# First row's broadcast load turned into columns of the small table, epsilon as a third group of the moments, padded token added by VectorE's multiplication

## The reference

```python
x = einsum(patches, conv_w) + conv_b            # 256 tokens of 128 per image, 2048 products each
for i in range(2):                              # two layers
    y = _ln(x); q, k, v = y @ qkv_w[i]          # layer norm, eps = 1e-5 under the root
    q = softmax(q, -1) * scale; k = softmax(k, -2)
    x = x + (q @ (k.T @ v)) @ out_w[i] + out_b[i]
    x = x + gelu(_ln(x) @ ff1_w[i] + ff1_b[i]) @ ff2_w[i] + ff2_b[i]
h = _ln(x) @ head_w + head_b                    # 192 wide
# linear attention of 12 heads, with one padded token whose phi(k) is 1 everywhere
z = 1 / (phi(q) . (sum of phi(k) over 256 tokens and the padded one) + EPS)
h = h + (q, kv, z) @ W_out + b_out              # of _layernorm(h)
h = h + proj(gelu(fc(_layernorm(h))))           # weights scaled by mixed alpha_e * alpha_r
```

## Time and profile before

| | us |
|---|---|
| median of three runs | 139.9 (138.65 to 140.72) |
| profiled execution, its own time | 139.65 |
| its span, first to last instruction | 137.9 |
| busy: TensorE products | 120.1 (87%), 938 instructions |
| busy: weight loads | 106.2 (77%) |
| busy: VectorE | 79.6 (58%), 231 instructions |
| busy: ScalarE | 66.6 (48%) |
| busy: GpSimd | 54.3 (39%), 65 instructions |
| mean granted TensorE clock | 0.975 of full |

### The profile page before, as it was taken

One profiled execution on the slowest core, in us unless ns is written; L12 is line 12 of the kernel. 1 busy time (PEld: TensorE's weight loads), 2 busy tenths in 40 slices (PEclk: granted clock), 3 DMA queues, 4 the chain that ended last, 5 costly groups with the idle time before them and its releaser, 6 DMA issues.

```text
span 137.9 us, 2475 instructions
## 1 busy us (share of the span) xinstructions
PE 120.1 (87%) x938; PEld 106.2 (77%) x938; DVE 79.6 (58%) x231; ACT 66.6 (48%) x149; POOL 54.3 (39%) x65
## 2 busy tenths in 40 slices
PE   6995699997899898998989989479984989999992
PEld 6985698796687686877777877269962878999991
DVE  0000406999579747795559944673858698356001
ACT  4000312951769966599667996028222140751420
POOL 0000270053649726587246764576293340022000
PEclk9999869999999999999999999977999999999999
DMA  4978999802950000000000000000000000000101
GB/s 127 392 297 324 409 415 410 309 11 84 324 127 0 0 2 5 0 0 5 0 0 0 0 7 0 0 0 2 5 0 0 0 0 0 0 5 0 57 0 57
DMA packets 4091, 11.63 MB, mean 84 GB/s; under 512 B 464, under 2 KB 1712, under 8 KB 4080
## 3 DMA queue, kind: packets, MB, share of 16 engines
q1 hardware_dynamic: 4080, 11.48, 23.0%
HBM read 11.09 MB, written 0.39 MB: 83 GB/s over the span
## 4 chain that ended last, share of the span: by engine, by line
PE 44%; DVE 31%; DMA 8%; issue 6%; POOL 5%; SPq 3%; ACT 2%; DVEq 0%; POOLq 0%
PE bank L329 14%; DMA patches_sb<-in_patches 8%; PE bank L596 5%; PE bank L487 4%; PE bank L463 4%; DVE nkmax L752 4%; DVE q L764 4%; DVE nqmax L759 4%; PE bank L353 3%; POOL qn L1157 3%; DVE xn L686 3%; PE bank L455 2%; DVE qsum L771 2%; SPq L278 2%; DVE ktok L780 2%
## 5 line engine op out<-in xcount | busy, mean ns | idle before, releaser
L1134 POOL TENSOR_TENSOR rstd<-var,minus_half 128x2 f32<-128x2 f32 x14 | 9.9, 705 | 44.8 <-DVE var L681 44.8
L1157 POOL TENSOR_TENSOR qn<-q,rqsum 128x512 f32<-128x512 f32 x8 | 8.2, 1042 | 10.5 <-DVE rqsum L776 10.5
L1011 ACT ACTIVATE kexp<-bank,nkmax 128x256 f32<-128x256 f32 x16 | 7.4, 471 | 7.2 <-DVE nkmax L752 6.9
L353 PE MATMUL bank<-embed_sb,patches_sb 128*128 128x128 f32 x64 | 9.6, 315 | 1.2 <-DMA patches_sb<-in_patches 1.2
L353 PEld LDWEIGHTS bank<-embed_sb,patches_sb 128*128 128x128 f32 x64 | 9.1, 227 | 1.4 <-DMA patches_sb<-in_patches 1.4
L353 PE MATMUL bank<-embed_sb 128*128 128x128 f32 x64 | 8.6, 294 | 1.5 <-DMA embed_sb<-in_embed 1.4
L463 PE MATMUL bank<-cw,qT 128*128 128x128 f32 x64 | 10.0, 288 | 0.0
L353 PEld LDWEIGHTS bank<-embed_sb 128*128 128x128 f32 x64 | 8.3, 207 | 2.0 <-DMA embed_sb<-in_embed 1.9
L463 PEld LDWEIGHTS bank<-cw,qT 128*128 128x128 f32 x64 | 8.2, 190 | 1.6 <-issue 0.8
L1006 ACT ACTIVATE qkvw_hi<-qkvw 128x512 fp32r<-128x512 f32 x3 | 1.9, 630 | 14.9 <-DMA qkvw<-in_qkv_w 14.9
L732 DVE TENSOR_TENSOR x<-bank,first_sb 128x128 f32<-128x128 f32 x4 | 1.0, 284 | 13.5 <-PE bank L353 13.5
(11 more groups left out here) (138 smaller groups left out, 333.5 us busy)
## 6 DMA issues: line engine op xcount, KB each, us to landing
patches_sb<-in_patches SPq DMA_DIRECT2D x4, 512.0 KB, 11.8
embed_sb<-in_embed SPq DMA_DIRECT2D x2, 768.0 KB, 6.3
restw<-in_rest_w SPq DMA_DIRECT2D x2, 768.0 KB, 14.1
embed_sb<-in_embed SPq DMA_DIRECT2D x2, 384.0 KB, 8.7
qkvw<-in_qkv_w SPq DMA_DIRECT2D x3, 256.0 KB, 10.6
embed_sb<-in_qkv_w SPq DMA_DIRECT2D x1, 768.0 KB, 4.5
embed_sb<-in_embed SPq DMA_DIRECT2D x1, 576.0 KB, 3.9
projw_raw<-in_proj_w SPq DMA_DIRECT2D x1, 576.0 KB, 14.8
```

What stands on the lines that cost most here:

```text
L353: mm = nc.tensor.matmul(EMB[i][t][:, 0:D], patches[:, t * P:(t + 1) * P], embed_sb[:, c, 0:D], start=(c == 0), stop=(c == KCONV - 1))
L1011: nc.scalar.activation(kexp[i][:, c, :], KB[c // 2][:, (c % 2) * TOKENS:(c % 2 + 1) * TOKENS], ACT.Exp, bias=nkmax[i][:, c:c + 1], accum_o ...
L1134: nc.gpsimd.tensor_tensor(rstd[i][:], var[i][:], minus_half[:], ALU.pow).then_inc(rstd_ready[i], 1)
L1157: nc.gpsimd.tensor_tensor(qn[i][:, t, :].rearrange("p (h d) -> p h d", h=HEADS), q[i][:, t, :].rearrange("p (h d) -> p h d", h=HEADS), rqs ...
```

## The change

Three edits. The row of 134 floats becomes 134 more columns of the small table, repeated on the host for each partition; the table grows from 248 to 382 columns, its load moves from after the sixth embed piece to after the fourth, and the broadcast load is gone. `bn_stats` writes into the first six of nine numbers a tile; the last three are a third group (count 0, mean 0, sum of squares width x epsilon), set once at the start in one buffer for each of the two widths, so that `bn_aggr` gives variance plus epsilon; the addition and its semaphore are gone, and GpSimd waits for `bn_aggr` itself. The one-row product is gone; VectorE computes (sum + 1) x q in one instruction.

```diff
-        small_sb = sb("small_sb", [P, P + EC + NCOL])
+        small_sb = sb("small_sb", [P, NSMALL])                  # NSMALL = P + EC + NCOL + NALPHA + D
-        first_sb = sb("first_sb", [P, NALPHA + D])
+        conv_b = small_sb[:, CONV_B_AT:NSMALL]
-        stats = per_image("stats", [P, TILES, 6])
+        stats = {D: per_image("stats", [P, TILES, 9]), E: per_image("stats3_", [P, TILES, 9])}
-        var = per_image("var", [P, TILES])
...
-                if j == CONV_PIECES - 2:
-                    sp.dma_start(first_sb[:], first_row.to_broadcast([P, NALPHA + D])).then_inc(loaded["first"], 16)
+                if j == CONV_PIECES - 3:
+                    sp.dma_start(small_sb[:], small).then_inc(loaded["small"], 16)
...
-            sp.dma_start(small_sb[:], small).then_inc(loaded["small"], 16)
...
                 for t in range(TILES):
-                    nc.tensor.matmul(KB[1][:, 0:E], ones[:, 0:P], qk3[i][:, t, E:2 * E],
-                                     start=(t == 0), stop=False)
-
-                nc.tensor.matmul(KB[1][:, 0:E], ones[0:1, 0:P], ones[0:1, 0:E],
-                                 start=False, stop=True).then_inc(ksum3_done, 1)
+                    mm = nc.tensor.matmul(KB[1][:, 0:E], ones[:, 0:P], qk3[i][:, t, E:2 * E],
+                                          start=(t == 0), stop=(t == TILES - 1))
+                mm.then_inc(ksum3_done, 1)
...
                 dve.wait_ge(ready, count)
+                if n == LN1(0) or n == LN3:
+                    dve.wait_ge(eps_set, 2 * IMAGES * TILES)
                 for t in range(TILES):
-                    nc.vector.bn_stats(stats[i][:, t, :], src[:, t, 0:width]).then_inc(moments[i], 1)
+                    nc.vector.bn_stats(stats[width][i][:, t, 0:6], src[:, t, 0:width]).then_inc(moments[i], 1)
                 for t in range(TILES):
                     dve.wait_ge(moments[i], 2 * TILES * n + t + 1)
-                    nc.vector.bn_aggr(mv[i][:, t, :], stats[i][:, t, :]).then_inc(moments[i], 1)
-                dve.wait_ge(moments[i], 2 * TILES * (n + 1))
-                nc.vector.tensor_scalar(var[i][:], mv[i][:, :, 1], EPS_LN, None, ALU.add).then_inc(var_ready[i], 1)
+                    nc.vector.bn_aggr(mv[i][:, t, :], stats[width][i][:, t, :]).then_inc(moments[i], 1)
...
-                nc.vector.tensor_tensor(qks3[i], qk3[i][:, :, 0:E],
-                                        KB[1][:, 0:E].unsqueeze(1).to_broadcast([P, TILES, E]),
-                                        ALU.mult).then_inc(z3_chain, 1)
+                nc.vector.scalar_tensor_tensor(out=qks3[i], in0=KB[1][:, 0:E].unsqueeze(1).to_broadcast([P, TILES, E]),
+                                               scalar=1.0, in1=qk3[i][:, :, 0:E], op0=ALU.add,
+                                               op1=ALU.mult).then_inc(z3_chain, 1)
...
+            for width in (D, E):
+                for i in range(IMAGES):
+                    nc.vector.memset(stats[width][i][:, :, 6:8], 0.0).then_inc(eps_set, 1)
+                    nc.vector.memset(stats[width][i][:, :, 8:9], width * EPS_LN).then_inc(eps_set, 1)
...
             def rsqrt(i, n):
-                pool.wait_ge(var_ready[i], n + 1)
-                nc.gpsimd.tensor_tensor(rstd[i][:], var[i][:], minus_half[:], ALU.pow).then_inc(rstd_ready[i], 1)
+                pool.wait_ge(moments[i], 2 * TILES * (n + 1))
+                nc.gpsimd.tensor_tensor(rstd[i][:], mv[i][:, :, 1], minus_half[:], ALU.pow).then_inc(rstd_ready[i], 1)
```

More of the change, by code:

```diff
@@ L78, with build @@
 NALPHA = len(EMBED) + len(RATIO)
-def build(nc, small, embed0, patches1, qkv_w, rest_w, rows, mix, first_row, fc_w, proj_w, head_w, aqkv_w, aout_w, out):
+ALPHA_AT = P + EC + NCOL
+CONV_B_AT = ALPHA_AT + NALPHA
+NSMALL = CONV_B_AT + D
+def build(nc, small, embed0, patches1, qkv_w, rest_w, rows, mix, fc_w, proj_w, head_w, aqkv_w, aout_w, out):
     with ExitStack() as ctx:
@@ L212, in build @@
         loaded = {n: sem(f"loaded_{n}") for n in (
-            ["small", "mix", "first", "rows", "fc", "proj", "head", "aqkv", "aout", "qkv1"]
+            ["small", "mix", "rows", "fc", "proj", "head", "aqkv", "aout", "qkv1"]
             + [f"embed{j}" for j in range(CONV_PIECES)] + [f"second{j}" for j in range(SECOND_PIECES)]
@@ L216, in build @@
         consts_set = sem("consts_set")
+        eps_set = sem("eps_set")
         table_loaded = sem("table_loaded")
@@ L224, in build @@
         x_ready = sems("x_ready")
-        moments, var_ready, rstd_ready, xn_ready, turned, yT_ready, yT_hi_ready, yT_lo_ready = (
-            sems(n) for n in ("moments", "var_ready", "rstd_ready", "xn_ready", "turned", "yT_ready",
+        moments, rstd_ready, xn_ready, turned, yT_ready, yT_hi_ready, yT_lo_ready = (
+            sems(n) for n in ("moments", "rstd_ready", "xn_ready", "turned", "yT_ready",
                               "yT_hi_ready", "yT_lo_ready"))
@@ L728, in x_from_conv @@
             def x_from_conv(i):
-                dve.wait_ge(loaded["first"], 16)
+                dve.wait_ge(loaded["small"], 16)
                 for t in range(TILES):
                     dve.wait_ge(conv_done, TILES * i + t + 1)
-                    last = nc.vector.tensor_tensor(x[i][:, t, :], EMB[i][t][:, 0:D], first_sb[:, NALPHA:], ALU.add)
+                    last = nc.vector.tensor_tensor(x[i][:, t, :], EMB[i][t][:, 0:D], conv_b, ALU.add)
                 last.then_inc(x_ready[i], 1)
             def mix_coefficients():
-                dve.wait_ge(loaded["first"], 16)
-                e, r = first_sb[:, 0:len(EMBED)], first_sb[:, len(EMBED):NALPHA]
+                dve.wait_ge(loaded["small"], 16)
+                e, r = small_sb[:, ALPHA_AT:ALPHA_AT + len(EMBED)], small_sb[:, ALPHA_AT + len(EMBED):CONV_B_AT]
                 shape = [P, len(EMBED), len(RATIO)]
@@ L1294 @@
     headmask[:EC] = np.kron(np.eye(EC // D3, dtype=np.float32), np.ones((D3, D3), np.float32))
-    small = np.concatenate([np.eye(P, dtype=np.float32), headmask, np.concatenate(cols).T], axis=1)
+    first_row = np.concatenate([a["L0_ffn_alpha_e"], a["L0_ffn_alpha_r"], a[T + "conv_b"]])
+    small = np.concatenate([np.eye(P, dtype=np.float32), headmask, np.concatenate(cols).T,
+                            np.broadcast_to(first_row, (P, NALPHA + D))], axis=1)
     rows = np.concatenate([a[T + "out_b"].reshape(-1), a[T + "ff2_b"].reshape(-1), a[T + "head_b"],
@@ L1312 @@
     masks[:, BIAS_MIX:] = mask_e[::SEG]
-    first_row = np.concatenate([a["L0_ffn_alpha_e"], a["L0_ffn_alpha_r"], a[T + "conv_b"]])[None]
     host = {
@@ L1316 @@
         "qkv_w": qkv_w, "rest_w": np.stack(rest), "rows": rows,
-        "mix": masks, "first_row": first_row,
+        "mix": masks,
         "fc_w": _chunks(a["L0_ffn_w_fc"].T, EC), "proj_w": _chunks(a["L0_ffn_w_proj"].T, P),
```

## The result

The changed kernel took 134.71 us (median of 4 runs, 134.61 to 134.86) against 139.28 us (4 runs, 137.66 to 140.72) for the kernel before: ratio 0.974, 95% interval 0.970 to 0.977. It is faster by 2.6%. The profiled execution spans 133.0 us, 4.9 less than before.

A forecast was written before the change was run, and what follows sets the result against it. Bound by bytes until 16 us, by VectorE and TensorE alternating in the tower, by TensorE from 91 us. Loads 1.35, clock 1.0, norms 0.55 and padded token 1.0 sum to 3.9 us: 136.0 us, range 134.9 to 138.5.

The forecast's parts named there:

- The loads: At the start, dropping the broadcast removes a DMA standstill from 9.5 to 11.5 us: 1.35 us, bounds 0 and 1.6.
- The clock: TensorE's clock no longer halves from 16 to 19.5 us: 1.0 us credited, bounds 0 and 1.5.
- Rival A: TensorE's clock falls all the same, decided from 14.5 to 18 us; the 1.0 credit is lost: 137.0 us, chance 0.21.
- The norms: Fourteen additions of 0.17 us leave VectorE and GpSimd starts sooner; together 0.55 us on the path.
- The piece at 85 us: The norm near 87 us, which TensorE waits for, was counted in full: 0.20 us.
- The steps up to 72 us: Norms at the end of steps 1 to 3, ahead of the transposes: 0.05 us each, 3 x 0.05.
- The pieces at 91 and 111 us: Two additions in VectorE's list ahead of what TensorE waits for: 0.1 us each, between 0 and 0.17.
- The padded token: Late attention in both images, without the one-row product: 1.0 us together, 0.5 if another wait takes over in the first.
- the two waits: VectorE's product starting 0.53 us late in the first image, the next product waiting 0.52 us in the second.
- The sum: Whole kernel: 1.35 + 1.0 + 0.55 + 1.0 = 3.9 us saved, giving 136.0 us for the median.
- Rival B: The slow stretch of loads is not the broadcast's, so the loads' change gives nothing: 138.35 us, chance 0.17.
- Rival C: The wider table, ahead of two embed pieces, passes at the slow rate and starves TensorE: 141.0 us, chance 0.05.

The follow-up runs named there:

- x4: Kernel before, its broadcast load reading 128 different rows of a table instead of one row 128 times: 137.18 against 139.0 us, ratio 0.987.
- x2: Kernel before with the norms' edit alone (third group in the moments, no addition of epsilon): 138.32 against 139.0 us, ratio 0.9945.
- x3: Kernel before with the padded token's edit alone (no one-row product, VectorE adds 1 and multiplies): 137.49 against 139.0 us, ratio 0.987.
- x6: Kernel before with five idle products in TensorE's two waits at the start, loads unchanged: 139.2 against 138.65 us, ratio 1.004.
- x10: Kernel before with idle products in TensorE's waits at the start, near 85 us and near 100 us: 137.51 us, ratio 0.986.
- x1: Kernel before with the loads' edit alone (wider small table after the fourth embed piece, no broadcast load): 136.88 against 139.0 us, ratio 0.985.
- x7: Changed kernel with four idle products near 85 us: 133.91 us against the kernel before's 138.65, ratio 0.968.
- x8: Changed kernel with the wide table's load moved behind the sixth embed piece: 134.58 us, ratio to the kernel before 0.973.
- x9: Changed kernel with eight idle products, four near 85 us and four near 100 us: 133.43 us, ratio to the kernel before 0.957.
- x11: Changed kernel repeated as it is, on the same chip as x12: 135.01 us, ratio to the kernel before 0.965.
- x12: x9's kernel repeated on the same chip as x11: 133.47 us, ratio to the kernel before 0.962.
- x5: Kernel before with the broadcast load issued twice, the second into an unread tile: 140.61 against 138.65 us, ratio 1.019.

## Why the prediction came out, step by step

**The loads, 1.35 us by bytes.** Right in cause, too small. x4 shows the cause by changing the source's addresses alone. The size: the first piece of image 1 lands at 15.77, 16.28, 16.13, 16.28 and 16.81 in the five traces with one broadcast load (before, x2, x3, x6, x10), mean 16.25, and at 14.21, 14.21, 13.92, 14.16, 13.61, 13.63, 14.88 and 14.16 in the eight without (after, x1, x4, x7, x8, x9, x11, x12), mean 14.10. The difference is 2.15 us; the medians of x1 and x4 at one stretch make it 1.8 and 1.7. The kernel before's own trace was the earliest of its kind; a price read from one execution's shortfall of bytes (546 KB) leaves that out, and leaves out the slower rates ahead of and behind the two microseconds that I took (328 to 383 GB/s from 8 to 9.5 us, 299 to 365 from 11.5 to 12.5). By the same reckoning over 8 to 12.5 us, the five traces fall short by 1.6 to 1.85 us. That the engines "stand still" is not borne out: in x2 they count as 95 to 100% busy at 93 and 196 GB/s.

**The clock, 1.0 us at the start.** The step that failed. The profiled execution had its fall at 16 us, and I took it for the usual one. Of the six traces with the broadcast load only that one has it: x2, x3 and x5 have none there with their waits left as they are, x6 and x10 none with filled waits, and filling those waits doesn't stop the second stretch (x6). In the traces that stretch is mostly a longer half-clock time near 90 us. It costs 1.2 us, and 28 of 56 runs of the kernel before had it (or more) against 1 of 16 of the changed one, x8 and x11 among them: worth some 0.5 us on average, half of what I credited, and for no reason that I gave. The loads' edit alone does not remove it (2 of 6 runs in x1, 3 of 6 in x4); why the changed kernel has it less often isn't settled. Rival A was to be decided at 14.5 to 18 us, where the clock stays full in the changed kernel, but as it does so in most traces with the broadcast load too, that decides nothing.

**The norms, 0.55 us.** 0.69 in the pair x10 and x9, 0.8 in x2's medians. The piece at 85 us was right to a hundredth (0.19). The steps up to 72 us gave 0.10 instead of 0.15. The pieces at 91 and 111 us, where the addition sat in VectorE's list, were 0.15 and 0.05 instead of 0.1 each (VectorE's next instruction starts 0.26 and 0.36 us after the first `bn_aggr` does, instead of 0.41 both times). Some 0.2 us lie in places where I had counted nothing, half of it between 72 and 86 us, half between 100 and 112. `bn_aggr`, taken at no cost, costs 0.01.

**The padded token, 1.0 us.** 0.51 + 0.51 + 0.15 in the pair: the sum had the two waits right and missed that the context product behind the second one gets shorter as well. VectorE's scalar came free, as the row of its neighbour said.

**The sum.** Without the clock I had 2.9 us and the runs have 4.1 (2.15 + 0.69 + 1.17 = 4.01 by the traces, 4.08 by the medians of x9 and x10). With the clock I had 3.9 and the first comparison has 4.6 by medians and 3.7 by its ratio. That the forecast came near is in part luck: three sizes too small, by 0.8, 0.15 and 0.15 us, and a clock credit too large by about 0.5 partly cancelled.

**Rival B** fell with x4. The Trainium skill's rule on it ("DMA: Bandwidth & Descriptors", Rules for kernel authors), that a leading broadcast of c copies confines a transfer to at most c engines when c is below 16, says nothing against 128 copies. x4 shows that a broadcast of a 536-byte row over 128 partitions costs time all the same. In the one window in which the row of 4,352 bytes passes, the rate is 422 GB/s; that the length of the row makes the difference was not tested by itself. **Rival C** did not occur: 386 GB/s from 3.5 to 8 us and 394 from 8 to 9.5, and x8 shows no cost of the place.

## What to carry to other kernels

A load of one short row into all partitions can cost, at a moment when loads are the bound, far more than its bytes (here 1.7 to 2.2 us for 67 KB, which take 0.17 at 404 GB/s): store the row once per partition, and append it to a table that is loaded anyway. Before crediting or debiting a clock fall to a wait, look at several executions: the mean clock of each run counts the falls, and the profiled one may have had its fall in an unusual place. Two kernels whose idle times are filled by unused products compare better: the runs of x9, x10 and x12 spread over 0.8 to 1.3 us, those of the kernel before beside them over 3.5 and 4.3.

## What was not expected of the hardware

In the microsecond from 9.5 us, with 128 reads of the same 536 bytes in the queue, 54 to 93 GB/s pass in the six traces that have them, with 128 reads of different ones 395 (x4). Half-clock time came in one piece of about 3.4 us (87.6 to 91.0 in the changed kernel) or in one of twice that (86.3 to 93.1 in x1), behind nearly the same activity: from 82 to 86 us TensorE is busy for 2.21 us in the one and 2.35 in the other. Products of no use in TensorE's waits, eight in x9 and x12 and thirteen in x10, kept the mean clock at 0.998 or more in all 18 runs.
